# Deeper buffers for the sorted rows and the residual, routing temporaries inside the row buffers, and one weight split moved, in a recurrent network followed by a mixture of experts

## What is computed

```python
shared = silu(x_flat @ shared_w1.T) @ shared_w2.T
top_k_gates, top_k_idx = jax.lax.top_k(x_flat @ gate_w.T, 2)
gates = zeros(T, 8).at[arange(T)[:, None], top_k_idx].set(softmax(top_k_gates))
h = einsum('td,ehd->teh', x_flat, experts_w1)
selected = einsum('ted,te->td', einsum('teh,edh->ted', silu(h), experts_w2), gates)
return x + shared + selected
```

## Time and profile before

| what | us |
|---|---|
| median of 3 runs | 389.0 |
| lowest and highest of them | 384.96, 389.73 |
| profiled execution, its own time | 387.75 |
| span of the profiled execution, first to last instruction | 385.9 |
| TensorE busy in it | 358.8 |
| ScalarE, VectorE, GpSimd busy | 243.9, 199.6, 109.2 |
| mean granted TensorE clock, share of full speed | 0.992 |

### The profile page before, as it was taken

The page is one execution under the profiler, slowest core; times in us unless marked ns, Lnnn a source line. Parts: engine busy times, 40 slices in busy tenths (PEclk is TensorE's granted clock), DMA queues, the critical chain, the costliest instruction groups (busy, mean ns, idle before and its releaser), DMA issues.

```text
span 385.9 us, 8917 instructions
## 1 busy us (share of the span) xinstructions
PE 358.8 (93%) x2458; PEld 253.2 (66%) x2459; DVE 199.6 (52%) x414; ACT 243.9 (63%) x478; POOL 109.2 (28%) x108
## 2 busy tenths in 40 slices
PE   5989999979997999798899999999999999999981
PEld 4758889945665676464566666666666666666661
DVE  0189999979986986783233333232333323233310
ACT  3777888868747766863455566655556665565630
POOL 0100001000275888500003334333223333222342
PEclk9999999989999999999999999999999999999998
DMA  7999999405696989877878899987889888888972
GB/s 201 422 430 429 426 402 349 155 3 110 115 226 153 210 186 242 178 148 152 154 170 153 162 166 171 165 155 148 150 144 155 158 147 158 142 155 141 164 138 29
DMA packets 158173, 73.94 MB, mean 192 GB/s; under 512 B 140736, under 2 KB 155200, under 8 KB 156992
## 3 DMA queue, kind: packets, MB, share of 16 engines
q1 hardware_dynamic: 151280, 64.27, 66.1%
q0 software_dynamic: 6864, 9.31, 16.1%
HBM read 23.68 MB, written 16.97 MB: 105 GB/s over the span
## 4 chain that ended last, share of the span: by engine, by line
PE 56%; DVE 16%; DMA 10%; issue 5%; ACT 5%; SPq 3%; another core or an unknown queue 1%; POOL 1%; ACTq 0%; DVEq 0%; POOLq 0%
PE py L1138 29%; PE z L1033 26%; DVE w_slots L544 8%; DVE w_slots L543 5%; DMA w_slots<-weights 4%; DMA space<-recurrence_w 4%; ACT space L891 2%; DVE chunk_bound L514 1%; DMA space<-space 1%; DMA space<-x_rows 1%; ACT w_slots L942 1%; ACT space L896 1%; ACT recurrence_w L896 1%; SPq L334 1%
## 5 line engine op out<-in xcount | busy, mean ns | idle before, releaser
L1138 PE MATMUL py<-w_slots,space 128*128 (+1 forms) x1272 | 148.4, 273 | 8.0 <-DMA space<-recurrence_w 4.8
L1033 PE MATMUL z<-w_slots,x 128*128 (+1 forms) x636 | 147.3, 382 | 4.8 <-DVE x L566 1.9
L1138 PEld LDWEIGHTS py<-w_slots,space 128*128 128x128 f16 x1272 | 123.8, 98 | 34.3 <-issue 9.5
L1033 PEld LDWEIGHTS z<-w_slots,x 128*128 128x128 f16 x636 | 62.3, 98 | 70.4 <-issue 5.6
L469 POOL DMA_INDIRECT out<-space x37 | 57.9, 1566 | 161.9 <-issue 69.5
L891 ACT ACTIVATE space<-z,tile_scales 128x512 f32<-128x512 f32 x106 | 71.8, 678 | 38.5 <-PE z L1033 30.0
L598 DVE SCALAR_TENSOR_TENSOR recurrence_w<-space,tile_scales,recurrence_w 128x512 f16<-128x512 f32 x54 | 40.2, 749 | 66.5 <-ACT recurrence_w L896 55.4
L598 DVE SCALAR_TENSOR_TENSOR space<-space,tile_scales 128x512 f16<-128x512 f32 x52 | 38.8, 750 | 53.1 <-ACT space L896 45.4
L544 DVE SCALAR_TENSOR_TENSOR w_slots<-w_slots,w_scale 128x1024 f16<-128x1024 f32 x36 | 46.2, 1283 | 1.3 <-ACT w_slots L942 0.3
L896 ACT ACTIVATE recurrence_w<-space,tile_scales 128x512 f16<-128x512 f32 x54 | 39.0, 722 | 11.9 <-ACT space L891 3.5
L896 ACT ACTIVATE space<-space,tile_scales 128x512 f16<-128x512 f32 x52 | 37.5, 722 | 7.8 <-ACT space L891 2.7
(11 more groups left out here) (114 smaller groups left out, 181.7 us busy)
## 6 DMA issues: line engine op xcount, KB each, us to landing
w_slots<-weights SPq DMA_DIRECT2D x9, 2048.0 KB, 28.8
sorted_rows<-pad_row SPq DMA_DIRECT2D x1, 5304.0 KB, 59.5
space<-x_rows SPq DMA_DIRECT2D x16, 128.0 KB
out<-space SPq DMA_DIRECT2D x16, 128.0 KB
space<-x_cols SPq DMA_DIRECT2D x1, 1024.0 KB, 8.2
space<-recurrence_w SPq DMA_TRANSPOSE x54
space<-space SPq DMA_TRANSPOSE x52
x<-sorted_rows SPq DMA_TRANSPOSE x39, 3.1
```

What stands on the lines that cost most here:

```text
L1033: last = nc.tensor.matmul(Z[u % 2][h][:], x16[:, u, x_part, k], weight(f, k * HID + h * BANK, BANK, part), start=k == 0 and x_part == 0 an ...
L1138: last = nc.tensor.matmul(PY[p][:, 0:D], hiddenT[:, p, low, q], weight(f, MATRIX + q * D, D, part), start=q == 0 and not low and part == 0 ...
```

## The change

Six things are done:
- `SORT_RING = 8` row buffers instead of four: `sort_row(t)` waits from t = 8 on, for the scatters of t - 8. For t = 4 it waits for `routed` (the end of the slots' computation) instead, since seven routing temporaries (`onehot` to `slot_of`) now lie in row buffers 4 to 7.
- A slot is `ROW = D + 4` = 260 f32 (1040 bytes), so that the memset of the tails and its semaphore go.
- The labels of row tiles 0 to 7 are written by one VectorE copy in `route_rows`, those of 8 to 15 by GpSimd as before, each behind the scatters of a tile four later than the buffer's last user.
- `x_res` has four buffers: four loads at g = 0, and store(g) loads x for tile g + 4.
- `EARLY_WIDES` falls from 23 to 22, so that piece 22 is split at g = 3, beside piece 23.
- `ys` and `magnitudes` lie elsewhere in `space`.

```diff
-ROW = D + 16
+ROW = D + META
+SORT_RING = 8
...
-EARLY_WIDES = 6 * WIDES - 1
+EARLY_WIDES = 6 * WIDES - 2
...
-        hr = carve(RING, ROW)
+        hr = carve(SORT_RING, ROW)
+        after_rows = at[0]
+        at[0] = RING * ROW
+        onehot = carve(TOP, TILES, E)
...
+        slot_of = carve(E, TILES)
+        assert at[0] <= after_rows
...
+        ys = carve(RING, D)
+        magnitudes = ys[:, 2:4].rearrange("p u d -> p (u d)").bitcast(BF16)
...
-        x_res = carve(2, D)
+        x_res = carve(RING, D)
...
-                if g + 2 < TILES:
-                    sp.dma_start(x_res[:, u % 2], x_tiles[g + 2]).then_inc(x_res_in[u % 2], 16)
+                if g + RING < TILES:
+                    sp.dma_start(x_res[:, u], x_tiles[g + RING]).then_inc(x_res_in[u], 16)
...
-                    for n in range(2):
+                    for n in range(RING):
                         sp.dma_start(x_res[:, n], x_tiles[n]).then_inc(x_res_in[n], 16)
...
-            nc.gpsimd.memset(hr[:, :, D + META:ROW], 0.0).then_inc(tails_ok, 1)
             pool.wait_ge(routed, 1)
-            for t in range(RING):
-                label(t)
             pool.wait_ge(padded, 16)
-            pool.wait_ge(tails_ok, 1)
             for t in range(TILES):
-                pool.wait_ge(row_copied, t + 1)
+                if t >= SORT_RING:
+                    pool.wait_ge(row_copied, t - SORT_RING + 1)
                 waited(row_ok, t + 1)
                 for k in range(TOP):
...
-                if 1 <= t and t - 1 + RING < TILES:
-                    waited(sorted_ok[(t - 1) % RING], 16 * TOP * ((t - 1) // RING + 1))
-                    label(t - 1 + RING)
+                if RING <= t < TILES - RING:
+                    u = t - RING
+                    waited(sorted_ok[u], 16 * TOP)
+                    nc.gpsimd.tensor_copy(hr[:, u, D:ROW], meta[:, u + SORT_RING]).then_inc(row_copied, 1)
...
                 link(last)
+                nc.vector.tensor_copy(hr[:, :, D:ROW], meta[:, 0:SORT_RING])
                 link(nc.vector.tensor_reduce(slots.rearrange("p k t -> p (k t)"), masked, AX.X, ALU.add))
...
-                if t >= RING:
-                    act.wait_ge(sorted_ok[t % RING], 16 * TOP * (t // RING))
+                if t == RING:
+                    act.wait_ge(routed, 1)
+                if t >= SORT_RING:
+                    act.wait_ge(sorted_ok[t % SORT_RING], 16 * TOP)
```

More of the change, by code:

```diff
@@ L171, in carve @@
             return v.rearrange("p (a b c) -> p a b c", a=shape[0], b=shape[1])
-        hr = carve(RING, ROW)
-        hr16 = hr.rearrange("p u r -> p (u r)").bitcast(F16).rearrange("p (u r) -> p u r", u=RING)
-        magnitudes = space[:, 0:CHUNK].bitcast(BF16)
+        hr = carve(SORT_RING, ROW)
+        hr16 = hr.rearrange("p u r -> p (u r)").bitcast(F16).rearrange("p (u r) -> p u r", u=SORT_RING)
+        after_rows = at[0]
+        at[0] = RING * ROW
+        onehot = carve(TOP, TILES, E)
+        picked = carve(TILES, E)
+        earlier = carve(E, TILES)
+        per_tile = carve(E, TILES)
+        running = carve(E, TILES)
+        restart = carve(E, TILES)
+        slot_of = carve(E, TILES)
+        assert at[0] <= after_rows
+        at[0] = after_rows
+        ys = carve(RING, D)
+        magnitudes = ys[:, 2:4].rearrange("p u d -> p (u d)").bitcast(BF16)
         hidden = carve(HID)
@@ L204, in build @@
         half_tanh = carve(TILES)
[L205 to L211, removed]
         masked = space[:, best_from:best_from + TOP * TILES * E].rearrange("p (t e) -> p t e", e=E)
@@ L235, in build @@
         bound_all_ok, split_ok, high_ok = sem("bound_all_ok"), sem("split_ok"), sem("high_ok")
-        x_res_in = [sem(f"x_res_in{u}") for u in range(2)]
+        x_res_in = [sem(f"x_res_in{u}") for u in range(RING)]
         xs_in = [sem(f"xs_in{u}") for u in range(RING)]
@@ L252, in build @@
             sem(n) for n in "x_hi_general x_lo_general up_mm_general logits_general".split())
-        tiles_ok, tails_ok = sem("tiles_ok"), sem("tails_ok")
+        tiles_ok = sem("tiles_ok")
         logits_mm, gap_ok, tanh_ok, picked_ok, prefix_mm, prefix_read, routed = (
@@ L262, in build @@
         row_mm, row_hi, row_ok, row_copied = sem("row_mm"), sem("row_hi"), sem("row_ok"), sem("row_copied")
-        sorted_ok = [sem(f"sorted_ok{u}") for u in range(RING)]
+        sorted_ok = [sem(f"sorted_ok{u}") for u in range(SORT_RING)]
         meta_in, idx_ok, idx_step = sem("meta_in"), sem("idx_ok"), sem("idx_step")
@@ L356, in _ @@
                 if g == TILES - 3:
-                    for u in range(RING):
-                        sp.wait_ge(sorted_ok[u], 16 * TOP * TILES // RING)
+                    for u in range(SORT_RING):
+                        sp.wait_ge(sorted_ok[u], 16 * TOP * TILES // SORT_RING)
                     load(0, 0)
@@ L604, in row_low @@
                 dve.wait_ge(row_hi, t + 1)
-                nc.vector.scalar_tensor_tensor(hr16[:, t % RING, D:2 * D], row_bank[t % 2][:, 0:D], STATE_SCALE,
-                                               hr16[:, t % RING, 0:D], ALU.mult, ALU.subtract).then_inc(row_ok, 1)
+                nc.vector.scalar_tensor_tensor(hr16[:, t % SORT_RING, D:2 * D], row_bank[t % 2][:, 0:D], STATE_SCALE,
+                                               hr16[:, t % SORT_RING, 0:D], ALU.mult, ALU.subtract).then_inc(row_ok, 1)
             def shared_y(g):
                 u = g % RING
-                dve.wait_ge(x_res_in[u % 2], 16 * (g // 2 + 1))
+                dve.wait_ge(x_res_in[u], 16 * (g // RING + 1))
                 if g >= RING:
@@ L613, in shared_y @@
                 dve.wait_ge(down_mm, g + 1)
[L614 removed]
+                nc.vector.scalar_tensor_tensor(ys[:, u], PY[u % 2][:, 0:D], tile_scales[:, g, 2:3], x_res[:, u],
                                                ALU.mult, ALU.add).then_inc(y_ok, 1)
```

7 lines of the change are left out of this document (2 added, 5 removed).

## The result

The changed kernel takes 382.5 us (median of four runs, 381.13 to 385.01); the kernel before, on the same chip, 388.99. The ratio is 0.9885 with a 95% interval of 0.984 to 0.993; the medians alone would give 0.983, or 6.5 us, from four runs each that spread over 4 to 5 us. Some executions of a kernel are slower than the rest, and the ratios are taken without them. On three further occasions, each with its own runs of before, it was 0.9918 [0.988, 0.996], 0.9932 [0.989, 0.998] and 0.9940 [0.990, 0.998]. So the change wins 0.6 to 1.2% by these ratios, 2.3 to 4.5 us, and not 2.3% (8.8 us, or 10.0 from the median of 389.0 to the predicted 379.0). The forecast was some two to four times too large by these ratios, on the right side.

A forecast was written before the change was run, and what follows sets the result against it. TensorE was taken as the bound, with 12.7 us lost before its dense expert stage. 1.9 - 0.5 + 5.0 - 0.3 + 3.2 = 9.3, less 0.5, gives 8.8 off 387.75: 379.0 us, range 377 to 382, over the cases 374 to 387.

The forecast's parts named there:

- I let it stand: From up(4) to up(12), 2.6 us lost to an unexplained ScalarE wait of 5.4 us; not counted as won.
- eight row buffers: ScalarE's three sort waits, 5.8 us, go; TensorE wins the early 3.2 us, up(12) to up(14); bounds 0 and 3.2.
- four x buffers: VectorE's residual x waits go, winning the late 5.0 us before up(19); extra loads at g = 0 cost 0.3.
- What bounds the kernel: TensorE, dense in the expert stage at 5.21 us a tile; only time lost before it, 12.7 us, can be won.
- Lost: 8.2: Up(12) to up(19) takes 44.7 us against 36.5 dense: 3.2 us lost early, 5.0 late.
- Piece 22 leaves, 1.9; it comes back, 0.5: Without the piece TensorE starts up(0) 1.9 us earlier; splitting it at g = 3 costs 0.5, bounds 0 and 2.1.
- Labels and memset: GpSimd has 8 copies fewer, VectorE one more; GpSimd's whole sort takes 52.5 us, ending at 155.7.
- Shorter slots: Rows at multiples of 16 bytes cost nothing, as loads have slack; value 0, bounds -0.2 and +1 us.
- The sort never became the bound: Rival: slower scatters make SP wait for all of them at g = 13; 394.5 us; chance 0.08.
- The gap moves: Rival: idle time moves to before down(0) and the clock falls behind it, 1.7 us lost; 381.2 us; chance 0.12.
- the x wasn't it: Rival: the late 5.0 us come from transposes before down(14) to down(17); only 3.8 us won, 384.0; chance 0.22.
- The 5.4 us go too: Rival: ScalarE's unexplained wait also goes, another 2.6 us won, the g = 3 split costs 1.0; 376.9; chance 0.15.

The follow-up runs named there:

- D's pair: Changed kernel with slots of 272 words and 23 early splits, against the same with 22, on one chip: 383.34 us (0.9923) against 384.13 (0.9893).
- the pair: For the slots: changed kernel with slots of 272 words against the changed kernel with 260, on one chip: 384.13 us (0.9893) against 385.85 (0.9932).

## Why the prediction was wrong

Two steps failed. The loss between up(4) and up(12), put at nothing ("I let it stand"), grew by 2.9 us; and the eight row buffers, put at 3.2 us won, won nothing in sum in the pairs (-1.6 and -2.5 us, 1.0 alone). A third was right in kind but too large: four x buffers, 5.0 us, measured 2.4 to 3.2. The first pair of traces, on chip A, shows it by stages: 0.4 us won up to up(4), 1.4 lost to up(12), 6.9 won to up(19), 0.6 lost to the last up(), 0.9 lost behind it, 4.4 in all. The prediction had 1.1, 0, 8.2, 0 and 0, less 0.5. Now its steps, one by one.

*What bounds the kernel.* Right: the expert stage lost about 1 us, with the slots, and what was won lies before it.

*The terms' source.* "Lost: 8.2" was read from one execution. Another has 41.7 - 36.5 = 5.2 us there, and the kernels with a single part changed have 3.6 to 4.4 (all on C). Up(12) to up(19) in four traces of the changed kernel averages 37.8 us, so 3.9 to 6.9 were won, and 1.3 over the dense 36.5 are left.

*Piece 22 leaves, 1.9; it comes back, 0.5.* The mechanism was right: up(0) starts 1.3 us earlier on average (80.9 over four traces against 82.25 over two), and up(4) 0.4 us earlier on A and 2.2 in D's pair. The kernel's time does not confirm the 1.4 us: undoing the step costs between -0.8 and 1.2 us where it was paired. The 0.19 us in front of up(0) were forecast as none.

*Four x buffers, 5.0, less 0.3.* The mechanism was right: L613's wait is gone, and it held TensorE back. The size is 2.4 to 3.2 on D and 1.9 to 2.7 alone on C. The step said "I put the whole late part to them"; a part of it was that execution's or that chip's. Up(14) to up(19), 31.1 us on A, takes 29.0 in the kernel before on D, 28.1 with two x buffers in the changed one there and 26.2 to 27.4 with four. Whether another part was covered by the ring's waits is not shown: the kernel before with four x buffers alone and with eight row buffers alone has 40.8 us from up(12) to up(19) with either, but on the same chip the one with nothing but shorter slots, and both waits, has 40.1.

*Eight row buffers, 3.2.* This step failed on the chips with late reports. The waits went as it said, but the time did not: -1.6 and -2.5 us in the two pairs against four in use, 1.0 alone in the kernel before. Its mechanism is real where nothing hides it: on B, without late reports, up(12) to up(14) is 3.5 us longer with four in use, close to the 3.2. On E the same stretch is dense with four and not with eight (10.42 and 11.66 us), and what was won or lost there went under in up(4) to up(12), 48.1 us with four and 50.0 with eight on average.

*"The 2.6 us I don't count as won... I let it stand."* It did not stand: up(4) to up(12) takes 50.5 us on average in the four traces of the changed kernel and 47.6 in the two of before. These 2.9 us were set at nothing in the forecast. Before and after the pauses came with late reports of TensorE, which come with the scatters; the step did not ask what caused them, nor whether a change of the sort could make them longer. Why they grew stays open: the pairs point to the ring, and two traces of the changed kernel on one chip differ by 4.1 us. That the ring did not cause the pause before row tile 4 fits the traces with eight, which have it too.

*Labels and memset.* As forecast, the mean scatter hardly changed, 1174 ns against 1191, and GpSimd's sort runs from 104.33 to 156.47 us, 52.1 against a forecast of 52.5. Page of the changed kernel, part 5:

```profile
L445 POOL DMA_INDIRECT sorted_rows<-space x32 | 37.6, 1174 | 18.5 <-issue 15.4
```

*Shorter slots, 0, bounds -0.2 and +1.* Undersized: 1.0 us in the expert stage alone, 1.5 to 1.7 in the pair. The reason given, that a load has slack for twice its time, held (no wait of L1035 for `sorted_rows` in the changed kernel's trace). What the higher share cost TensorE instead, here and there, no run names.

Added up by the pairs: x 1.9 to 3.2, the ring -2.5 to 1.0, the piece -0.8 to 1.2, the slots -1.7 to -0.9. The ends add up to -3.1 and 4.5 us, the middle is 0.7, and 2.3 to 4.5 were measured; the steps are not strictly additive, and the pairs have errors of about 1.5 to 2.5 us each. So the parts do not account for the whole with any sharpness.

*The rivals.* The sort never became the bound: SP shows no wait for scatters in the changed kernel's trace. The clock did not fall behind the new gaps. "The gap moves" (381.2) and "the x wasn't it" (384.0) gave the times nearest to 382.5, both for reasons that the runs speak against; that is luck. "The 5.4 us go too" went the opposite way. The measured 382.5 lies within the range over the cases, 374 to 387, and just outside the forecast's own, 377 to 382.

## What to carry to other kernels

A wait that is removed is worth what its bottleneck engine gains, and that is read by pairs on one chip: here 17.5 us of VectorE's waits were worth 2 to 3, and 5.8 us of ScalarE's nothing in two pairs, though on a third chip the trace shows that they cost TensorE 3.5. Before a stretch's loss is made a term of a sum, look whether a second execution has it; here two differed by 3 us. And a pause that the trace can't name belongs into the forecast with a price of its own: this one grew by 2.9 us when it was left at nothing. Where DMA engines are busy most of the time, measure a new row pitch by itself: slots 4% shorter raised the share from 0.88 to 0.92.

## What the runs showed of the hardware

Of some 45 end reports of TensorE between 100 and 160 us, 14 to 27 came over 0.5 us late, many of them 1 to 5 us, while GpSimd issued indirect DMAs at one in 1.3 to 1.5 us, on four chips of five; with the scatters 14 us later, on one of them, the lateness moved along (first at 120.3 us instead of 109). Nothing of the kind appears in the expert stage, with one indirect DMA in 5.2 us, beyond single reports.

The same kernel before takes 384.1 us on one chip and 387 to 389 on four. The traces of four variants on that one chip have no late reports; that this makes the difference in time is likely but not shown. Comparisons across chips mislead by as much as this change was worth.

Slots at a pitch of 1040 bytes instead of 1088 raise the DMA engines' share from 195 to 355 us from between 0.87 and 0.89 to between 0.91 and 0.94, at 152 to 156 GB/s either way.
